# A delta-rule recurrence whose prediction products go from 64 of 32 rows to 16 of 128 rows, with the state spread block-diagonally by 16 transfers per tile

## The reference, cut to what matters

```
rk = heads(x) / |heads(x)|          # key of this position
wk = rk of the position before
v  = x Wv^T;  g, b = sigmoid(x Wg^T), sigmoid(x Wb^T)
each t:  pred = wk_t . S
         err  = (v_t - pred) * b_t
         S    = S + wk_t (x) err     # S: 32 x 32 per batch and head
         o_t  = (rk_t . S) * g_t
out = o Wo^T
```

## Time and profile before

| | |
|---|---|
| median of 3 runs | 2370.92 us (2365.35 to 2374.8) |
| profiled execution | 2373.69 us |
| its span | 2372.0 us |
| PE busy | 2108.6 us (89%) |
| DVE busy | 1985.7 us (84%) |
| ACT busy | 1727.6 us (73%) |
| POOL busy | 1726.7 us (73%) |
| mean granted PE clock | 0.966 |

### The profile page before, as it was taken

The page is one execution under the profiler, slowest core; times in us unless marked ns, Lnnn a source line. Parts: engine busy times, 40 slices in busy tenths (PEclk is TensorE's granted clock), DMA queues, the critical chain, the costliest instruction groups (busy, mean ns, idle before and its releaser), DMA issues. The chain is left out here.

```text
span 2372.0 us, 145909 instructions
## 1 busy us (share of the span) xinstructions
PE 2108.6 (89%) x61992; PEld 1334.4 (56%) x61992; DVE 1985.7 (84%) x5810; ACT 1727.6 (73%) x3628; POOL 1726.7 (73%) x3098
## 2 busy tenths in 40 slices
PE   1679999999999999999999999999999988499997
PEld 1355666566666665656666656666666655255554
DVE  5487899888898888988898888989988985488886
ACT  3767777777777777777777777877777743477775
POOL 2667888888888888888888888888888853144343
PEclk7789999999999999999999999999999997799999
DMA  2111222222222222222222222222222211478885
GB/s 86 51 43 58 76 79 77 75 75 76 78 77 75 74 76 75 76 75 76 76 78 77 75 75 77 78 75 77 77 80 77 59 61 49 151 196 231 227 229 131
DMA packets 132139, 215.53 MB, mean 91 GB/s; under 512 B 31353, under 2 KB 31361, under 8 KB 131489
## 3 DMA queue, kind: packets, MB, share of 16 engines
q1 hardware_dynamic: 131488, 206.20, 30.0%
HBM read 104.40 MB, written 67.11 MB: 72 GB/s over the span
## 5 line engine op out<-in xcount | busy, mean ns | idle before, releaser
L775 DVE TENSOR_TENSOR ps_elim<-ps_elim,sys 128x30 f32<-128x30 f32 (+14 forms) x1920 | 543.6, 326 | 0.8
L783 DVE TENSOR_TENSOR sys<-sys,ps_elim 128x30 f32<-128x30 f32 (+14 forms) x1920 | 534.8, 316 | 1.0
L900 PE MATMUL ps_v<-wv,xt 128*128 128x512 f16 x1536 | 429.7, 390 | 26.1 <-DMA kbd<-kt 13.5
L900 PE MATMUL ps_y<-wo,ot 128*128 128x512 f16 x1536 | 406.9, 388 | 11.6 <-DVE x L827 9.5
L927 PEld LDWEIGHTS ps_chain<-rhs,t_t 32*32 32x32 f32 x16384 | 263.4, 144 | 132.9 <-issue 131.6
L927 PE MATMUL ps_chain<-rhs,t_t 32*32 32x32 f32 x16384 | 296.1, 218 | 24.3 <-issue 18.4
L684 ACT ACTIVATE state<-ps_s 128x512 f32<-128x512 f32 x128 | 76.5, 598 | 265.0 <-PE ps_s L991 265.0
L921 PEld LDWEIGHTS ps_chain<-state,key_t 32*32 32x32 f32 x16384 | 174.8, 105 | 152.6 <-issue 151.1
L991 PEld LDWEIGHTS ps_s<-err,key_b 32*32 32x32 f32 x16384 | 172.6, 107 | 142.9 <-issue 142.3
L1277 PE MATMUL ps_f<-wq,f_xq 128*128 128x512 f16 x1024 | 242.6, 381 | 6.7 <-DVE f_xq L1243 6.7
L803 DVE TENSOR_TENSOR rhs<-val,ps_chain 128x512 f32<-128x512 f32 x128 | 88.0, 687 | 188.3 <-PE ps_chain L921 187.7
(11 more groups left out here) (159 smaller groups left out, 5072.2 us busy)
## 6 DMA issues: line engine op xcount, KB each, us to landing
x_in<-in_L_attn_x SPq DMA_DIRECT2D x128, 256.0 KB
kbd<-kt SPq DMA_DIRECT2D x512, 64.0 KB, 2.0
x_res<-in_L_attn_x SPq DMA_DIRECT2D x128, 256.0 KB
x_scratch<-x SPq DMA_DIRECT2D x128, 256.0 KB, 6.4
f_x<-x_scratch SPq DMA_DIRECT2D x32, 1024.0 KB, 7.7
out<-f_res SPq DMA_DIRECT2D x128, 256.0 KB, 3.8
gate<-gates SPq DMA_DIRECT2D x128, 7.9 KB
gate<-gates SPq DMA_DIRECT2D x128, 0.2 KB
```

The costliest lines, as they stand in the source:

```text
L775: dve.tensor_tensor(tmp, factors(r, c, first, end)[:, c - first:C - 1 - first, c - first:c - first + 1].to_broadcast(shape), sys[:, r, c:c ...
L783: dve.tensor_tensor(dst, dst, tmp, ALU.add).then_inc(elim_done[r], 1)
L900: last = pe.matmul(out, lhs[:, a, kb, :], weights[:, w, kb, :], start=(i == 0), stop=(i == 3 * KB - 1))
```

## The change

`predict` no longer multiplies 64 blocks of 32 x 32. For each of 4 groups of heads and each batch it makes one product of 128 contracted rows: `kt` (4 heads x 32) against `state_bd`, in which the 32 x 32 states of the 4 heads stand on the diagonal of a 128 x 128 block. `state_bd` is zeroed once. For each tile the copy `state` is spread into it by 16 transfers, one for each batch and block, which SP issues when ACT has copied the state. VectorE's `key_t` is gone, and `kt` gets 8 buffers. `predict` is now in one piece, behind five value matmuls, and `chain_ready` waits for the transfers (eight semaphores, two for each batch). One output piece between the two halves of `update` shrinks from three matmuls to one. The two loads and the second gate transfer move within SP's list, and x_res gets four buffers. One scratch tile is shared, and some semaphores of the feed-forward part are merged; VectorE sets one small tile there.

```diff
@@ sync, one step @@
+                n, l, live = on(base, j, LAG_GRAM - 1)
+                if live:
+                    wait(sp, s["gate_moved"], n * 16 + 16)
+                    if isinstance(n, int) and n == 0:
+                        sp.wait_ge(s["zeros"], 3)
+                    sp.dma_start(gate[0:P:C, l, :], gates[C - 1:P:C, (l - 1) % 8, H:2 * H]).then_inc(gate_done[l], 16)
...
+                                     kt[HD * i:HD * i + HD, l, :, :]).then_inc(kbd_loaded[l % 2], 16)
+                n, l, live = on(base, j, 0)
+                if live and n < NT - 1:
+                    wait(sp, s["state_done"], n + 1)
+                    for b in range(B):
+                        for i in range(HB):
+                            w = KB * HD * i
+                            sp.dma_start(state_bd[HD * i:HD * i + HD, b, i, :],
+                                         state[C * b:C * b + C, w:w + KB * HD]).then_inc(state_loaded[b][l % 2], 16)
@@ gpsimd @@
-            pool.memset(state[:, 0, :], 0.0).then_inc(s["state_done"], 1)
-            pool.memset(kbd[:, :, :, :, :], 0.0).then_inc(s["kbd_zero"], 1)
-            pool.memset(gates[:, BODY - 1, :], 0.0).then_inc(s["first_gate"], 1)
+            pool.memset(state_bd[:, :, :, :], 0.0).then_inc(s["zeros"], 1)
+            pool.memset(kbd[:, :, :, :, :], 0.0).then_inc(s["zeros"], 1)
+            pool.memset(gates[:, BODY - 1, :], 0.0).then_inc(s["zeros"], 1)
@@ scalar @@
                     wait(act, s["s_psum"], n + 1)
-                    wait(act, s["pred_psum"], n)
-                    nc.scalar.activation(state[:, (l + 1) % 2, :], ps_s[:, :], ACT.Copy).then_inc(s["state_done"], 1)
+                    wait(act, s["pred_psum"], n + 1)
+                    nc.scalar.activation(state[:, :], ps_s[:, :], ACT.Copy).then_inc(s["state_done"], 1)
@@ vector @@
-                n, l, live = on(base, j, LAG_V)
-                if live:
-                    wait(dve, s["key_done"], n + 1)
-                    wait(dve, s["pred_psum"], n - 7)
-                    wait(dve, s["gram_psum"], n - 7)
-                    dve.transpose(key_t[:, l, :, :], heads(key[:, l % 2, :])).then_inc(s["keyt_done"], 1)
@@ tensor @@
                     wait(pe, s["err_done"], n)
-                    wait(pe, s["state_done"], n + 1)
-                    wait(pe, s["keyt_done"], n + 1)
+                    wait(pe, s["kt_done"], n + 1)
+                    if n == 0:
+                        pe.wait_ge(s["zeros"], 3)
+                    else:
+                        for b in range(B):
+                            pe.wait_ge(state_loaded[b][(n - 1) % 2], 64 * ((n - 1) // 2 + 1))
...
-                def predict(half):
+                def predict():
                     if live:
-                        for h, q, e in blocks(half):
-                            last = pe.matmul(ps_chain[q, e], key_t[q, l, h, :], state[q, l % 2, e], start=True, stop=True)
+                        for g in range(KB):
+                            for b in range(B):
+                                q, w = slice(C * b, C * b + C), slice(P * g, P * g + P)
+                                moving = state_bd[:, b, :, HD * g:HD * g + HD]
+                                last = pe.matmul(ps_chain[q, w], kt[:, l, g, q], moving, start=True, stop=True)
                         return last
...
-                predict(0)
...
-                value(0, SHARE)
-                last = predict(1)
+                value(0, 2 * SHARE - 1)
+                chain_ready(base, j)
+                value(2 * SHARE - 1, 2 * SHARE)
+                last = predict()
...
                 update(0)
-                output(SHARE, 2 * SHARE)
+                output(SHARE, SHARE + 1)
                 last = update(1)
...
-                output(2 * SHARE, WHOLE - 1)
-                if y_live:
-                    chain_ready(base, j + 1)
-                last = output(WHOLE - 1, WHOLE)
+                last = output(SHARE + 1, WHOLE)
```

More of the change, by code:

```diff
@@ L288, in attention @@
         ln_sc = sb("ln_sc", [P, 2, 4])
[L289 removed]
+        unread = {(n, m): sb(f"unread_{n}_{m}", [P, D]) for n, m in (("ln", "sum"), ("ln", "var"), ("y", "var"))}
         x_hat = sb("x_hat", [P, 4, D])
@@ L316, in attention @@
         err = sb("err", [P, 2, D])
-        state = sb("state", [P, 2, D])
+        state = sb("state", [P, D])
+        state_bd = sb("state_bd", [P, B, HB, KB * HD])
         pred = sb("pred", [P, D])
@@ L431, in step @@
                     sp.dma_start(gate[1:P, l, :], gates[0:P - 1, l, H:2 * H]).then_inc(s["gate_moved"], 16)
[L432 to L435, removed]
-                n, l, live = on(base, j, LAG_V)
-                if live:
[L438 to L443, removed]
                 n, l, live = on(base, j, LAG_Y)
                 if live:
-                    wait(sp, s["x1_done"], n - 1)
-                    sp.dma_start(tile(x_res, l % 2), rows(io["x"], base, j, LAG_Y)).then_inc(res_loaded[l % 2], 16)
+                    wait(sp, s["x1_done"], n - 3)
+                    sp.dma_start(tile(x_res, l % 4), rows(io["x"], base, j, LAG_Y)).then_inc(res_loaded[l % 4], 16)
                 n, l, live = on(base, j, LAG_STATS2)
@@ L452, in step @@
                                  x1[:, l % 4, :]).then_inc(x1_stored[l % 4], 16)
+                n, l, live = on(base, j, LAG_V)
+                if live:
+                    if isinstance(n, int) and n == 0:
+                        sp.wait_ge(s["zeros"], 3)
+                    wait(sp, s["kt_done"], n + 1)
+                    for i in range(HB):
+                        sp.dma_start(kbd[HD * i:HD * i + HD, l % 2, i, :, :],
+                                     kt[HD * i:HD * i + HD, l, :, :]).then_inc(kbd_loaded[l % 2], 16)
[3 more added lines that the diff above has]
+                    for b in range(B):
+                        for i in range(HB):
+                            w = KB * HD * i
+                            sp.dma_start(state_bd[HD * i:HD * i + HD, b, i, :],
+                                         state[C * b:C * b + C, w:w + KB * HD]).then_inc(state_loaded[b][l % 2], 16)
             run(step)
@@ L928, in solve_error @@
                         return last
-                if live and not on(base, j - 1, LAG_Y)[2]:
-                    chain_ready(base, j)
-                predict(0)
                 if v_live:
@@ L947, in step @@
                             out = ps_gram[q, :].rearrange("p (i h) -> p h i", h=H)[:, HB * g:HB * g + HB, :]
-                            last = pe.matmul(out, kt[:, m_l % 2, g, q], kbd[:, m_l % 2, :, g, q], start=True, stop=True)
+                            last = pe.matmul(out, kt[:, m_l, g, q], kbd[:, m_l % 2, :, g, q], start=True, stop=True)
                     last.then_inc(s["gram_psum"], 1)
@@ L990, in update @@
                         for h, q, e in blocks(half):
-                            last = pe.matmul(ps_s[q, e], key_b[q, l, e], err[q, l % 2, e],
+                            col = HD * (h % HB * KB + h // HB)
+                            last = pe.matmul(ps_s[q, col:col + HD], key_b[q, l, e], err[q, l % 2, e],
                                              start=(isinstance(n, int) and n == 0 and h == 0), stop=True, skip_group_check=True)
```

53 lines of the change are left out of this document (26 added, 27 removed).

## The result

The changed kernel takes 3630.35 us (median of 4 runs, 3624.2 to 3635.07) against 2369.65 us before: 1.532 times, 95% interval 1.528 to 1.536. The forecast was 3490, range 3120 to 3760.

The account below looks back on a forecast made before the run. PE was taken as the bound at 14.81 us per tile. The change would make it 13.1 + 10.7 = 23.8 us, 1080 us over 120 tiles plus 42 for the last seven, so 3490 us, 80% range 3120 to 3760.

Parts of the forecast that it names:

- The bound and the hidden round trip: Before the change PE sets the 14.81 us tile, and the state's round trip through ACT is hidden with 1.3 us spare.
- Issue, 0.63 us: SP issues transfers one after the other at 0.63 us each, bounds 0.29 and 0.75, with length mattering little.
- The walk round the loop: One tile from the end of update to the next: 13.1 us until PE resumes, then 10.7, together 23.8.
- Up to PE's resuming: Twenty issues in one go on SP, then 2.16 us landing: PE resumes 13.1 us after update ends, idle for 9.3.
- The low clock: After each long wait PE's value matmul and gram run at 1.2 GHz, 1.1 us extra per tile.
- From gram to T0: PE's work from gram's end to the end of update: 7.38 us less 0.50 moved, plus 0.4 for stalls.
- Freed on PE, 0.36 to 0.6 us per tile: Sixteen products in predict take 1.02 us instead of 1.38, saving 0.36 us per tile, and fewer stalls may save 0.2.
- Hidden transfers: Rival, 3%: transfers land before PE arrives and the kernel is faster, 2295 us; SP's issues alone set a 2500 us floor.
- Fast small issues: Rival, 12%: the sixteen small transfers issue at 0.29 us each, a tile takes 18.7 us, the whole 2870 us.
- PE at 1.2 GHz through the chain: Rival, 6%: PE keeps the low clock through the chain part, 3.5 us more per tile, 3930 us.
- No queue is late: SP needs 15.8 of 23.8 us per tile, so x_in, x_res and the store still have 8 us to spare.
- SP's moved gate transfer: The second gate transfer moves to SP's next step; the forecast passed over this edit and gave it no cost.

Follow-up runs that it names:

- e2_quarter_bytes: The changed kernel with each of the sixteen transfers moving 32 of its 128 columns, 128 B rows instead of 512 B: 3622.57 us.
- e1_eight_transfers: The changed kernel with eight state transfers per tile instead of sixteen, so batches 2 and 3 are never brought in: 3014.67 us.
- e7_no_transfer: The changed kernel without its sixteen transfers; predict multiplies a spread state that stays zero and waits for ACT's copy: 2242.68 us, 0.944 of before.
- e6_split_gate: The kernel before plus sixteen transfers per tile that nobody reads, with the second gate transfer moved to the head of the next step's list: 3094.98 us.
- e5_unwaited: The kernel before plus sixteen extra transfers per tile, issued by SP into a tile that nobody reads: 3328.48 us.
- e8_copies: The changed kernel with its sixteen transfers replaced by copies out of PSUM, eight by ACT and eight by VectorE: 2459.84 us, 1.035 of before.
- e9_copies_12_4: The changed kernel with copies for transfers, 12 by ACT and 4 by VectorE, ACT's gate exponent between its two groups: 2611.17 us, 1.094 of before.

## Why the prediction was right

*The bound and the hidden round trip*: right. What had 1.3 us to spare now needs 13.

*Issue, 0.63 us*: right. The sixteen took 10.09 us, and e2_quarter_bytes and e1_eight_transfers show that count and not size sets it.

*The walk round the loop*, from the starts of the rows, averaged over 108 tiles between 300 and 3000 us:

| from | to | forecast, us | measured, us |
|---|---|---|---|
| T0 | PE resumes | 13.1 | 13.4 |
| PE resumes | end of gram | 3.4 | 3.9 |
| end of gram | next T0 | 7.3 | 7.6 |
| whole tile | | 23.8 | 24.8 |

*Up to PE's resuming*, three errors nearly cancel. SP begins at T0 - 1.5, not T0 - 1.0. The issues stretch: 3.0 us for the four of `kbd` where I had 2.5 (in the step shown the fourth takes 1.63 us where 0.59 is usual), and 10.35 for the sixteen. The landing is shorter, 1.92 us from the start of the last issue where I had 2.16. That PE's idle time came out as I said, 9.28 us (1011.1 us in 109 tiles) for 9.3, is partly luck: PE arrives 0.3 us later than I had it, and its wait ends 0.3 later.

*The low clock*: the largest error of the sum. Value matmul, `predict` and gram take 3.87 us, and 2.20 at the full clock in e7_no_transfer: it costs 1.7 us where I charged 1.1. I had taken the recovery from a stage with 1.9 us of idleness, and read 2 to 2.5 us of it; here the granted clock stays at 0.50 for 4.1 us of work on average (2.7 to 6.1), which covers most of gram: 1.65 us for 0.99.

*From gram to T0*, 0.3 us more than I had: the rows take 7.3 us on average where I had read 6.9 from one step, and the stalls are 0.3 for the 0.4 charged. 127 tiles times 0.97 (24.77 less 23.8) is 123 us, which is nearly the whole of 3630 less 3490.

*Freed on PE, 0.36 to 0.6 us per tile*: too small, 0.95 in e7_no_transfer. I had read `predict` as 1.38 us from one step, where it took 1.93 on average with its stalls, and the new form as 1.02, where it takes 0.89 start to start. It did not matter to the sum.

*Rivals.* Hidden transfers: excluded, none of the sixteen issues took under 0.5 us; its floor of 2500 us from SP alone was too low, e6_split_gate gives 3095 with nobody waiting for the landing, since issues stretch behind loads of 256 KB. Fast small issues: excluded by e2_quarter_bytes, whose 128 B rows took 0.63 us each. The Trainium skill's 50 ns of dispatch, which I had cited for the first rival ("DMA: Bandwidth & Descriptors", "Anatomy of one DMA — SWDGE (gpsimd) path"), is a twelfth of that; that section is on transfers issued by GpSimd, and all of these come from SP. PE at 1.2 GHz through the chain: no, but it stayed there for 4.1 us on average where I had 2 to 2.5.

*No queue is late*: right for the changed kernel, where SP still waits 584.4 us in 109 tiles, 5.4 each, for ACT's copy of `kt` (I had 8 us to spare). *SP's moved gate transfer* I had costed at nothing in silence; behind enough issues it is worth 234 us, the difference of e5_unwaited and e6_split_gate. What it is worth in the changed kernel no run shows.

## What to carry to other kernels

A transfer has a price on the queue that issues it, here 0.63 us for rows of 512 B as for rows of 128 B, and N of them inside a recurrence cost N times that: count issues before bytes. Before work is moved onto an engine that seems to have slack, follow the loops through its in-order list: ACT had 20% to spare and could not take three microseconds at that place. A saving on the busiest engine can be real (5.6% here) and still be bought with a round trip that costs ten times as much.

## What the runs showed of the hardware

- SP and ACT issue transfers at the same time without slowing one another: 5.03 and 5.29 us for eight each.
- An issue soon behind a 256 KB load can take several microseconds: x_res, issued 1.9 us after x_in, took 0.8 to 4.2 us in the changed kernel, 3.1 as a rule, where 0.60 is usual before. In e6_split_gate it was the first `kbd` issue, 3.2 us, and x_res behind it took 0.62. The held issue ended 5.2 and 5.4 us on average after x_in's had begun; where x_res came 5.9 us behind x_in (e8_copies) it took 0.8. I had not expected it; what holds it was not tried.
- A copy of 32 x 128 fp32 across partition blocks takes 0.27 us on ACT and 0.29 on VectorE out of PSUM. Out of SBUF VectorE took 0.22 as a rule, but 0.97 on average in 118 of 776 copies, which all began while POOL was at work on `pred` or `o_g`.
- PE's "issue" stalls end 1.1 to 1.6 us after a 16 KB transfer of the queue of kind "instruction", of which there is one for every 256 matmuls and weight loads. They are 1.2 us per tile in the four groups with 64 products in one piece, 0.7 with two pieces of 32, 0.4 with 16 products.
- In e9_copies_12_4 the granted clock falls to 0.50 behind only 2.07 us without work on PE (mean over the steady stretch 0.91).
